# The last eight pairs of a conditioned residual kernel: loaded and computed pair by pair instead of two pairs at a time

## The reference

```
x = x + einsum('bct,bcd->bdt', x, W0[itok_B_0_15])
x = x + einsum('bct,bcd->bdt', x, W1[itok_B_0_31]) + transpose(b[itok_B_0_31])
```

## Time and profile before

| | us |
|---|---|
| median of 3 runs | 651.86 (650.8 to 653.19) |
| profiled execution, its own time | 651.78 |
| its span, first to last instruction | 648.8 |
| TensorE busy | 563.7 (87%) |
| VectorE / ScalarE / GpSimd busy | 378.1 / 363.6 / 159.1 |
| DMA, mean over the span | 419 GB/s |
| mean granted TensorE clock | 0.946 of full speed |

### The profile page before, as it was taken

One profiled execution on the slowest core, in us unless ns is written; L12 is line 12 of the kernel. 1 busy time (PEld: TensorE's weight loads), 2 busy tenths in 40 slices (PEclk: granted clock), 3 DMA queues, 4 the chain that ended last, 5 costly groups with the idle time before them and its releaser, 6 DMA issues.

```text
span 648.8 us, 11443 instructions
## 1 busy us (share of the span) xinstructions
PE 563.7 (87%) x4706; PEld 252.8 (39%) x4706; DVE 378.1 (58%) x486; ACT 363.6 (56%) x515; POOL 159.1 (25%) x301
## 2 busy tenths in 40 slices
PE   1899999798989799798899798989889978979896
PEld 1344444343434344343344343434334433434342
DVE  1166667555756647466647557646565654665563
ACT  0366666555656646456646556546565654665563
POOL 2222522023330323312233311332302333021201
PEclk9999999898989989889989889979899997999899
DMA  8999999999999999999999999999999999999957
GB/s 361 432 413 430 427 435 417 432 419 430 431 416 431 428 426 433 433 430 442 420 433 429 434 432 434 428 430 429 435 438 428 425 442 422 429 412 417 426 236 314
DMA packets 15424, 271.93 MB, mean 419 GB/s; under 512 B 2133, under 2 KB 2166, under 8 KB 2230
## 3 DMA queue, kind: packets, MB, share of 16 engines
q1 hardware_dynamic: 5616, 137.37, 49.6%
q10 hardware_dynamic: 5510, 76.19, 27.7%
q0 software_dynamic: 4272, 58.07, 21.1%
HBM read 137.40 MB, written 134.22 MB: 419 GB/s over the span
## 4 chain that ended last, share of the span: by engine, by line
issue 54%; PE 16%; POOL 14%; DMA 11%; POOLq 3%; DVE 1%; ACT 0%; ACTq 0%; DVEq 0%; SPq 0%
PE acc L275 11%; POOL map0T_sb L218 7%; POOL map L231 6%; DMA xt<-in_x_dram 5%; DMA out_dram<-xt 4%; PE acc L282 2%; POOLq L208 2%; PE acc L270 2%; DMA cond_rep<-in_conds_dram 2%; PE acc L387 1%; POOLq L205 1%; POOLq L218 1%; POOLq L231 0%; POOL out_dram L200 0%; DVE xt L426 0%
## 5 line engine op out<-in xcount | busy, mean ns | idle before, releaser
L282 PE MATMUL acc<-xt,both 32*128 32x512 f32 x3456 | 441.4, 636 | 42.5 <-DMA xt<-in_x_dram 42.5
L485 ACT ACTIVATE xt<-acc,bias_of 64x512 f32<-64x512 f32 x432 | 294.5, 682 | 179.7 <-PE acc L282 175.6
L282 PEld LDWEIGHTS acc<-xt,both 32*128 32x128 f32 x3456 | 188.1, 198 | 278.9 <-issue 168.8
L424 DVE TENSOR_SCALAR xt<-acc,bias_of 64x512 f32<-64x512 f32 x216 | 160.5, 743 | 206.2 <-PE acc L282 204.6
L426 DVE TENSOR_SCALAR xt<-acc,bias_of 64x512 f32<-64x512 f32 x216 | 163.2, 755 | 3.1
L200 POOL DMA_DIRECT2D out_dram<-xt x27 | 15.7, 581 | 387.4 <-DVE xt L426 387.4
L218 POOL TENSOR_TENSOR map0T_sb<-w0T_sb,ident 128x128 f32<-128x128 f32 x108 | 71.2, 660 | 35.4 <-issue 21.4
L275 PE MATMUL acc<-xt,both 64*128 64x512 f32 x320 | 75.0, 616 | 2.0 <-ACT both L474 2.0
L231 POOL TENSOR_TENSOR map<-w_sb,ident 128x128 f32<-128x128 f32 x126 | 63.9, 507 | 0.0
L477 ACT ACTIVATE xt<-acc,bias_of 64x1024 f32<-64x1024 f32 x36 | 39.9, 1109 | 32.6 <-PE acc L275 32.2
L275 PEld LDWEIGHTS acc<-xt,both 64*128 64x128 f32 x320 | 31.4, 194 | 40.7 <-issue 37.5
(11 more groups left out here) (37 smaller groups left out, 33.5 us busy)
## 6 DMA issues: line engine op xcount, KB each, us to landing
xt<-in_x_dram SPq DMA_DIRECT2D x27, 4096.0 KB, 28.3
out_dram<-xt ACTq DMA_DIRECT2D x36, 2048.0 KB, 26.5
out_dram<-xt POOLq DMA_DIRECT2D x27, 2048.0 KB, 25.2
xt<-in_x_dram SPq DMA_DIRECT2D x10, 2048.0 KB, 29.4
w_sb<-in_w_dram SPq DMA_DIRECT2D x1, 2048.0 KB, 9.3
w0T_sb<-in_w0T_dram SPq DMA_DIRECT2D x1, 1024.0 KB, 4.8
out_dram<-last POOLq DMA_DIRECT2D x2, 512.0 KB, 5.0
out_dram<-last POOLq DMA_DIRECT2D x2, 192.0 KB, 3.7
```

The source lines that it names most:

```text
L282: return nc.tensor.matmul((acc0, acc1)[k % 2][:, at:at + CHUNK], both_quad[k * QC:(k + 1) * QC, buf, u, :], xt_quad[k * QC:(k + 1) * QC, s ...
L424: nc.vector.tensor_scalar(xt[0:HC, q % SLOTS + p, j * CHUNK:(j + 1) * CHUNK], acc0[0:HC, at:at + CHUNK], bias[0:HC, :], None, ALU.add)
L485: out = nc.scalar.activation(xt[HC:C, q % SLOTS + p, v * T + j * CHUNK:v * T + (j + 1) * CHUNK], acc1[v * HC:(v + 1) * HC, at:at + CHUNK], ...
```

## The change

Pairs 56 to 63 are units of one pair; pairs 8 to 55 stay in twos. So SyncE issues six 2 MB loads in place of the three 4 MB loads of pairs 56 to 61. TensorE runs two quads (pairs 52 to 55) and eight pairs after the loop, which makes one turn less. ACT stores pairs 56 to 62; POOL, which stored pairs 57, 59 and 61, stores nothing there and keeps only its pieces of pair 63. The final waits of ACT count accordingly. `pair`, `quad`, `combine` and the evictions are unchanged.

```diff
-    units = [(q, 1) for q in range(SLOTS)] + [(q, 2) for q in range(SLOTS, PAIRS - 2, 2)] + [(PAIRS - 2, 1), (PAIRS - 1, 1)]
+    units = [(q, 1 if q < SLOTS or q >= PAIRS - SLOTS else 2) for q in range(PAIRS) if q < SLOTS or q >= PAIRS - SLOTS or q % 2 == 0]
...
-            with pe.Fori(1, TURNS - 1) as now:
+            with pe.Fori(1, TURNS - 2) as now:
...
-            quad(4, 0, 2 * TURNS, (TURNS - 1) * LOAD, SLOTS - 2, 1, TURNS)
-            pair(SLOTS - 2, 1, 2 * TURNS, 2 * LOAD, SLOTS - 1, 1, 2)
-            pair(SLOTS - 1, 0, 2 * TURNS, 2 * LOAD, 0, 0, 0)
+            quad(4, 0, 2 * TURNS - 2, (TURNS - 2) * LOAD, 6, 2, TURNS - 1)
+            quad(6, 1, 2 * TURNS - 2, (TURNS - 2) * LOAD, 0, 1, TURNS)
+
+            for s in range(SLOTS - 1):
+                pair(s, s % 2, 2 * TURNS, 2 * LOAD, s + 1, 1, 2 if s % 2 == 0 else TURNS)
+            pair(SLOTS - 1, 1, 2 * TURNS, 2 * LOAD, 0, 0, 0)
...
-                act.wait_ge(stored[q], LOAD * (TURNS if q % 2 == 0 else 1))
+                act.wait_ge(stored[q], LOAD * (TURNS if q % 2 == 0 else 2 if q < SLOTS - 1 else 1))
             for g in range(SLOTS // 2):
-                act.wait_ge(stored_pool[g], LOAD * (TURNS - 1 if g < SLOTS // 2 - 1 else TURNS - 2))
+                act.wait_ge(stored_pool[g], LOAD * (TURNS - 2))
```

## The result

The changed kernel takes 654.31 us (median of 20 runs, 651.62 to 657.14) against 651.04 for the kernel before (20 runs, 648.42 to 655.91): ratio 1.0044, 95% interval 1.0027 to 1.0061. By the ratio it is slower by 0.4%, 2.9 us; the two medians are 3.3 apart. The profiled execution took 654.23 with a span of 652.1, 3.3 more than the 648.8 of before. A few executions of a kernel are some per cent slower than the rest of the same kernel, and the ratios leave those out.

The account below looks back on a forecast made before the run. A closed loop of loads and stores bounds the kernel up to the last units; the end is pair 63's start plus 19.5 us. Later start +0.2 and clock +1.0 on 651.78 give 653.0 us, range 650.2 to 655.8.

Parts of the forecast that it names:

- clock price of 1.0: Pair 63's first matmuls, after a wait for its load: a fall of the granted clock, taken as +1.0 us, bounds 0 and 2.9.
- within 0.3%: Whole kernel: the time differs from before by no more than about 0.3%, 2 us; chance 0.51.
- What bounds the end: The end is the start of pair 63 plus 19.5 us, and that start hangs on a load's landing.
- The turns by packet: DMA engines: each busy queue sends one packet in its turn; a 16 KB packet takes 0.61 us, a two-pair load's is 32 KB.
- load 58 at 580.6: Pair 58's load, sharing with the stores of pairs 54 and 55 for 14.7 us, was to land at 580.6.
- 3 turns left ... 548.2: Stores of pairs 50 and 51: 3 turns left at 542.7, 5.5 us with three packets a turn, so slots free at 548.2.
- pair 63 starting within 1 us of 629.3: Sign that the forecast holds: pair 63 starts about when it did before, 629.5 against 629.3, +0.2 us.
- The slower rival: The clock falls in pair 63's first matmuls after its wait for a load: +2.8 to +4.0 us, 654.6 to 655.8; chance 0.33.
- Edits costed at nothing: Single-pair evictions, POOL's maps, three more loads issued by SyncE and three more stores by ACT: all hidden, no time added.
- The faster rivals: Last loads get more than their turns, last landing 627.1, -2.2 us, 649.6; or row size doesn't matter, 643.6; together chance 0.14.
- the case of a half share whatever the rows: SyncE's queue has half of the engines always: 2 MB loads 9.8 us apart from 542.7, total 643.6; part of 0.14.
- A fixed cost for each load: Three more loads cost 3.2 us each beyond their bytes: +9.6 us, 661; chance 0.02.

Follow-up runs that it names:

- e3_pool: The changed kernel with pairs 57, 59 and 61 stored by POOL again, ACT storing 56, 58, 60 and 62: 655.46 us, 1.0053 of the kernel before.
- e1_rows16: The kernel before with only the loads of pairs 56 to 61 each issued as two DMAs with 16 KB rows: 653.04 us, 1.0016 of the kernel before.
- e6_b_store8_56: The kernel before with ACT's and POOL's stores of pairs 56 to 62 as two DMAs of 8 KB rows: 648.04 us, 0.9961 of the kernel before.
- e4_last4: Half of the change: pairs 60 to 63 single, 8 to 59 in twos: 654.58 us, 1.0036 of the kernel before.
- e2_store8: The changed kernel with ACT's stores of pairs 56 to 62 as two DMAs of 8 KB rows: 647.1 us, 0.9922 of the kernel before.
- e9_load8: The changed kernel with the loads of pairs 56 to 63 as two DMAs of 8 KB rows: 659.47 us, 1.0121 of the kernel before.
- e5_act: The kernel before with the second pair of each two-pair unit stored by ACT too, none by POOL: six runs, 664.3 to 677.1 us, no ratio.

## Why the prediction was right or wrong

The time of 654.31 lies in the range (650.2 to 655.8), 1.3 us above the forecast of 653.0. That it came so near is partly luck: the change was forecast as +1.2 us and is +2.9, and a clock price of 1.0 that was never paid covers part of a landing forecast too early. The likeliest case was "within 0.3%"; the measured 0.44% (0.27 to 0.61) falls into the case that had 0.35. Point by point:

- **What bounds the end** was right: pair 63's start plus a fixed tail. Start 632.06, span 652.1: the tail is 20.0 instead of 19.5, 0.24 of it in pair 63's own matmuls (7.57 against two thirds of 11.00).
- **The turns by packet** held where they were tested: loads 9.8 us apart one to one, 7.4 and 9.9 with small store rows, and both edits of row size moved the time the way that was stated, by more than was stated (-7.2 against -3 to -5, +5.2 against +1 to +5). e3_pool and the price in e1_rows16 were overestimated.
- **The term that was mis-sized: load 58 at 580.6.** It landed at 582.9, and the five steps of 9.8 behind it were right (632.0 - 582.9 = 49.1 against 48.9). The step that failed is the first: "3 turns left ... 548.2", taken from one profile. SyncE's releases show it, line 180 of the changed kernel, loads of pairs 58 and 59:

```profile
L180 SPq DMA_DIRECT2D xt<-in_x_dram x1: 327/327/327, 550.2 to 550.2; - x1
...
L180 SPq DMA_DIRECT2D xt<-in_x_dram x1: 327/327/327, 552.1 to 552.1; - x1
```

The stores of pairs 50 and 51 ended at 550.2 and 552.1, 4 and 5 turns after 542.7: 3 packets more, 1.8 us, and the rest, 0.5, is within the 0.3 us a stretch that I had named as a bound. The three turns were the state of one execution: in two other kernels that are alike up to there, with turns of 2.44 us, those stores needed 9.9 us (e6_b_store8_56, 4 turns) and 12.5 us (e4_last4, 5 turns). The gap before pair 54's store, in which load 57's last five packets were to go alone, was not there either: ACT issued that store at 564.70, before pair 52's had landed (565.1). In all, +2.8 stands where I had +0.2, and the sign "pair 63 starting within 1 us of 629.3" failed.
- **TensorE's waits** from pair 58 on were 5.00, none, 0.73, 1.44, 1.40 and 1.41 us, where 1 to 2 before each was forecast.
- **The clock** was wrong in this profile and in its repetition: waits of 1.4 us ahead of pair 63 and no fall (x32 in 7.57 and 7.56). The +1.0 was not paid. The slower rival had the right sign and the wrong cause; its price of 2.8 to 4.0 us met the measured change only because the landing was late. That the cost exists e3_pool shows, with 1.7 us after a wait of 2.02. "It decides from a last wait of about 1.2 us" was not borne out, and the kernel before already spoke against it, with 2.82 us and no fall:

```profile
522.99 6.29 PE L282 MATMUL acc<-xt,both 32*128 32x512 f32 x56 [2.82 <-DMA xt<-in_x_dram]
```

- **Edits costed at nothing** cost nothing that can be seen: pairs ran at 8.1 us when their loads were there, and ACT's three more stores made no difference (e3_pool).
- **The faster rivals**: row size plays its part (e2_store8, e9_load8), so the case of a half share whatever the rows is dead.
- **A fixed cost for each load** is dead too: the loads landed 9.8 us apart, which their packets explain, and seven transfers more in e2_store8 went with a gain. The 2.0 us that the prediction takes from the Trainium skill (DMA: Bandwidth & Descriptors, "Anatomy of one DMA — SWDGE (gpsimd) path") is a figure for transfers that GpSimd issues; the loads here are SyncE's.

## What to carry to other kernels

When loads and stores saturated the DMA engines together, they shared by packets (rows of 8, 16 and 32 KB here), so the row size of each transfer and the number of busy queues said who went first. Making the loads of the last stage smaller took bandwidth from them exactly where they had become critical; halving the rows of the stores beside them gave a kernel 0.7 to 0.8% faster than the old one for a few lines. To forecast such an end, count what the slowest engine sends before the last load over the whole run, and not from the state of its queues at one moment of one profile: one store more gives 630.7 here, the count from 542.7 gave 629.5, measured are 632.0 and 631.4.

## What the runs showed of the hardware

**One store queue is slower than two.** With all stores of two-pair units on ACT's queue, the mean of a stretch in the middle of e5_act is

```profile
535.00:599.00 64.00, 54.86 (x484) 24.34 (x484) 35.37 (x49) 33.90 (x51) 10.73 (x20) 0.89 0.98 392
```

392 GB/s (the last number), where the kernel before has 427 in 443:602, at engines 98% busy. It is the load rows that take longer: one of 32 KB takes 1.39 us in the mean there and 1.23 in the kernel before, a store row 0.61 to 0.62 in both. Loads come sooner, 20.3 us from issue in the median where the earlier trace rows's kernel has 28.3, but the second store of a unit takes 40.5 and frees its slot late. One engine still trails: of the 16 completions of such a second store the trace has 15 by 580.7 and the last at 599.0. POOL's queue carried nothing then, so an engine trails without it, which speaks against the guess in the Trainium skill (DMA: Bandwidth & Descriptors, "Latency and other measured facts"); whether it is one of the two engines that the section calls slower, no row tells. Why the load rows take longer, and why that engine trails, is open.

**The turn is one row.** The Trainium skill (same page, "Queues, rings and completion order") lets an engine drain a packet of about 9 to 17 descriptors from a queue before it changes. The trace of before doesn't agree. Its trailing engine is nearly alone around 617 to 622: its packets of 16 KB start 0.6 us apart and go q1, q10, q0, q1, q10, q0, one row each (617.35, 617.96, 618.58, 619.22, 619.83, 620.45). In the changed kernel, once only the trailing engine still loads, the eight rows of the last load start 1.21 to 1.24 us apart, from 621.74 to 630.32: one store row between each two. The shares in the earlier trace rows alone don't tell, since turns of any equal number of rows give them too.
